# Attention with mxfp4 gate on one core: transposes moved from TensorE to DMA, scores two steps ahead, mask and maximum in one operation

## What is computed

```
xn = layernorm(x)
q, k, v = split(xn @ Wqkv.T + b)            # 16 q heads, 8 k heads, v as 4 x 256, head size 128
p1 = softmax(causal(q[...,0] k[...,0]^T / sqrt(128)));  p2 = the same with the odd heads
p = p1 - lam * p2                            # lam from four vectors and lam0
o = p @ v;  o = o * rsqrt(mean(o*o) + eps) * subln * (1 - lam0)
s = o @ out_w.T + out_b
g = silu(quant(xn) @ quant(ffn_w).T + ffn_b) # quant: mxfp4, blocks of 32
out = x + s * g
```

## Time and profile before

| | us |
|---|---|
| median of 3 runs | 1835.9 (1833.76 to 1836.29) |
| the profiled execution, whole | 1837.28 |
| its span | 1835.5 |
| granted TensorE clock, mean | 0.977 |
| one batch of 32 steps in the middle | 213.50 |
| PE, DVE, ACT, POOL busy | 1678.7, 1269.1, 964.5, 710.0 |

### The profile page before, as it was taken

One profiled execution on the slowest core, in us unless ns is written; L12 is line 12 of the kernel. 1 busy time (PEld: TensorE's weight loads), 2 busy tenths in 40 slices (PEclk: granted clock), 3 DMA queues, 4 the chain that ended last, 5 costly groups with the idle time before them and its releaser, 6 DMA issues.

```text
span 1835.5 us, 29927 instructions
## 1 busy us (share of the span) xinstructions
PE 1678.7 (91%) x10545; PEld 1039.1 (57%) x10577; DVE 1269.1 (69%) x2829; ACT 964.5 (53%) x2642; POOL 710.0 (39%) x1442
## 2 busy tenths in 40 slices
PE   3568999999899999999999999999989999999988
PEld 2345565556655565556655566555655566556654
DVE  4668888548874688648884588646885488845772
ACT  4554566436653566436664366534664366634661
POOL 2214553226422463225532364224632255323243
PEclk7879999999999999999999999999999999999999
DMA  7300000100000000100001000010001000000001
GB/s 258 92 24 1 1 1 1 52 18 1 1 30 30 12 1 1 41 24 7 1 4 49 18 2 1 29 35 7 1 1 41 24 7 1 7 24 24 1 1 40
DMA packets 20680, 42.04 MB, mean 23 GB/s; under 512 B 1682, under 2 KB 2228, under 8 KB 20532
## 3 DMA queue, kind: packets, MB, share of 16 engines
q1 hardware_dynamic: 20532, 40.13, 6.5%
HBM read 31.74 MB, written 8.39 MB: 22 GB/s over the span
## 4 chain that ended last, share of the span: by engine, by line
PE 37%; DVE 28%; ACT 15%; issue 12%; POOL 6%; DMA 0%; SPq 0%; POOLq 0%; DVEq 0%; ACTq 0%
PE ps L418 11%; PE ps L420 10%; PE ps L419 10%; ACT pp L654 9%; DVE negmax L922 6%; DVE pp L937 4%; DVE qkv L879 4%; DVE ps L920 2%; DVE coef L935 2%; DVE ebias L925 1%; ACT qkv L632 1%; PE ps L542 1%; PE ps L474 1%; DVE v L889 1%; PE ps L476 1%
## 5 line engine op out<-in xcount | busy, mean ns | idle before, releaser
L654 ACT ACTIVATE pp<-ps,ebias,ssc 128x384 f32<-128x384 f32 (+3 forms) x512 | 312.1, 614 | 289.2 <-DVE ebias L925 229.7
L418 PE MATMUL ps<-xT,wqkv 128*128 128x512 f16 x768 | 295.2, 384 | 8.5 <-DVE qkv L879 5.3
L419 PE MATMUL ps<-xT,wqkv 128*128 128x512 f16 x768 | 294.4, 383 | 0.0
L420 PE MATMUL ps<-xT,wqkv 128*128 128x512 f16 x768 | 294.3, 383 | 0.0
L700 ACT ACTIVATE junk<-ps 128x256 bf16<-128x256 f32 x256 | 98.0, 383 | 270.4 <-PE ps L420 270.3
L418 PE MATMUL ps<-qkv,pT 128*128 128x256 f16 x640 | 175.2, 274 | 56.8 <-issue 41.0
L922 DVE TENSOR_REDUCE negmax<-ps 128x2 f32<-128x256 f32 (+3 forms) x256 | 211.1, 824 | 8.8
L911 DVE SCALAR_TENSOR_TENSOR res<-ps,small,obias 128x512 f32<-128x512 f32 x32 | 24.0, 751 | 249.0 <-PE ps L420 249.0
L418 PE MATMUL ps<-wout,heads 128*128 128x512 f16 x512 | 194.0, 379 | 0.0
L419 PE MATMUL ps<-wout,heads 128*128 128x512 f16 x512 | 194.0, 379 | 0.0
L420 PE MATMUL ps<-wout,heads 128*128 128x512 f16 x512 | 194.0, 379 | 0.0
(11 more groups left out here) (150 smaller groups left out, 3768.0 us busy)
## 6 DMA issues: line engine op xcount, KB each, us to landing
xin<-in_L_attn_hidden_states SPq DMA_DIRECT2D x8, 1024.0 KB, 5.3
xres<-in_L_attn_hidden_states SPq DMA_DIRECT2D x32, 256.0 KB, 2.8
out_x<-res SPq DMA_DIRECT2D x32, 256.0 KB, 2.0
qkv<-in_L_attn_Wqkv_w SPq DMA_DIRECT2D x8, 512.0 KB, 9.7
heads<-in_L_attn_Wqkv_w SPq DMA_DIRECT2D x8, 512.0 KB, 11.5
qkv<-in_L_attn_out_w SPq DMA_DIRECT2D x4, 512.0 KB, 3.8
heads<-in_L_attn_out_w SPq DMA_DIRECT2D x4, 512.0 KB, 3.6
gate<-in_L_ffn_weight SPq DMA_DIRECT2D x1, 1024.0 KB, 13.2
```

Of the source, the lines that this page charges most:

```text
L418: mm(out, ah, bh, start=start and j == 0, stop=False)
L419: mm(out, ah, bl, start=False, stop=False)
L420: last = mm(out, al, bh, start=False, stop=stop and j == n - 1)
L654: run(pp[:, m, 0:w], sc_ps[:, m, 0:w], ACT.Exp, bias=ebias[:, m:m + 1], scale=ssc[:, c:c + 1], accum_out=psum_l[:, s % 2, m:m + 1]).then_i ...
```

## The change

Six things are done together.

1. TensorE turns neither the map nor the output. The combined map is split in two fp16 parts first (`ph`: high on ACT, low on DVE, from SBUF), and SP issues a transposing DMA of 128 x 2w fp16 elements into `pT`. The output is also split first (`on`: high and low, the low part a new DVE operation each step), and a second transposing DMA of 128 x 512 fp16 elements puts it into `oT`. The copies from PSUM of the turned output (L663, L943) are gone. 512 transposing DMAs of 64 to 256 KB stand in SP's queue, two a step.
2. Scores run two steps ahead instead of one. The two banks that held the turned map and output are a second scores buffer.
3. Mask, scale and maximum are one DVE operation per map (two a step), with a bf16 mask as wide as the map: `tensor_tensor_reduce`, which the build turns into two instructions each, the second a 128x1 write of the result.
4. The second exponential is written back over its scores in PSUM, and `combine` reads it there.
5. Row sums, norms and square sums have two or four buffers; POOL forms its first two norm values two steps ahead.
6. The gate's t1, t2 buffers are replaced by `gate` and `v32`, so the v fill also waits for the gate. Stores and residual loads have fixed places between the transposing DMAs on SP.

```diff
-            def maxima(g, s, step):
-                diag = sc_ps[:, :, w - P:w]
-                tt(diag, diag, mask[:].unsqueeze(1).broadcast_to([P, 2, P]), ALU.add).then_inc(mask_done, 1)
-                nc.vector.tensor_reduce(out=negmax[:], in_=sc_ps[:, :, 0:w], axis=AX.X, op=ALU.max, negate=True)
-                tt(ebias[:], negmax[:], ssc[:, c:c + 2], ALU.mult).then_inc(ebias_done, 1)
+            def maxima(n, m):
+                dve.wait_ge(scores_done, n + 1)
+                sc = sc_ps[u][:, m, 0:w]
+                nc.vector.tensor_tensor_reduce(sc, sc, mask[:, S - w:S], ssc[:, c:c + 1], BIG, ALU.add, ALU.min,
+                                               ebias[:, u, m:m + 1]).then_inc(max_done, 1)
...
+            def transpose_p(n):
+                w = place(n)[3]
+                wait(sp, ph_lo, n + 1)
+                wait(sp, pv_done, n - 1)
+                sp.dma_start_transpose(pT[:, n % 2, 0:2 * w // P, :], ph[:, n % 2, 0:2 * w])\
+                  .then_inc(pT_done[n % 2], 16)
+            def transpose_o(n):
+                wait(sp, on_lo, n + 1)
+                sp.dma_start_transpose(oT[:, c:c + 2, :, i * P:(i + 1) * P].rearrange("p c s t -> p (c s) t"),
+                                       on[:, h].rearrange("p c s t -> p (c s t)")).then_inc(oT_done[h], 16)
...
+            for n in range(NSTEPS):                       # PE
+                if n + 2 < NSTEPS:
+                    scores(n + 2)
+                for f in PLAN[n]:
+                    fill(f)
+                attend(n)
...
+            for n in range(NSTEPS):                       # ACT
+                if n:
+                    square_o(n - 1)
+                if n + 1 < NSTEPS:
+                    p_hi(n + 1)
+                if n:
+                    normalised(n - 1)
+                if n + 2 < NSTEPS:
+                    exps(n + 2)
+                for f in PLAN[n]:
+                    fill(f)
...
+            for n in range(NSTEPS):                       # DVE
+                    combine(n + 1)
+                    maxima(n + 2, 1)
+                    p_lo(n + 1)
+                    maxima(n + 2, 0)
+                prepare_some(b, s, 0)
+                    normalised_lo(n - 1)
+                prepare_some(b, s, 1)
+                for f in PLAN[n]:
+                    fill(f)
+                prepare_some(b, s, 2)
```

More of the change, by code:

```diff
@@ L108, with plan, place, fill_of @@
 PROLOGUE = [("xT", 0, k) for k in range(NT)] + [(kind, 0, j) for kind, j in PROJ]
[L109 to L113, removed]
+Fill = namedtuple("Fill", "kind g j n hi v ffn gate out")
+def plan():
+    n = hi = v = ffn = 0
+    rows = []
+    for b in range(-1, B):
+        steps = schedule(b > 0, b < B - 1) if b >= 0 else [PROLOGUE]
+        for step in steps:
+            row = []
+            for kind, g, j in step:
+                gate = 4 * b + j
+                out = 4 * b + (j if kind == "last" else j - NT)
+                row.append(Fill(kind, g, j, n, hi, v, ffn, gate, out))
+                n += 1
+                hi += kind in ("q", "k", "xT")
+                v += kind == "v"
+                ffn += kind == "ffn"
+            rows.append(row)
+    return rows[0], rows[1:], n
+FIRST, PLAN, FILLS = plan()
+assert len(FIRST) % 2 == 0
+END = [Fill("out", 0, k, FILLS + k - (NT - 2), 0, 0, 0, 0, (B - 1) * NT + k) for k in (NT - 2, NT - 1)]
+NSTEPS = B * NS
+def place(n):
+    return n // NS, n % NS // STEPS, n % STEPS, (n % STEPS // 2 + 1) * P
+def fill_of(kind, b, g, j):
+    rows = [FIRST, *PLAN]
+    lo = max(0, b * NS + 1 - (NS // 4 if g == 0 and kind in ("q", "k", "v", "xT") else 0) - (2 if kind == "xT" else 0))
+    for row in rows[lo:lo + NS + NS // 4]:
+        for f in row:
+            if (f.kind, f.g, f.j) == (kind, g, j):
+                return f.n
+    raise KeyError((kind, b, g, j))
 WB = 2 * NC * G
@@ L130, in setup_order @@
             i += 1
[L131 to L157, removed]
+    return order + [("fill", m) for m in range(i, len(PROLOGUE))] + [("scores", 0)] + [("o", n) for n in range(OB)] \
+        + [("ahead", 0)]
 def build(nc, x_d, wqkv_d, bqkv_d, lq1_d, lk1_d, lq2_d, lk2_d, sub_d, ow_d, ob_d, fw_d, fb_d, out_d):
@@ L407, in _ @@
+            transpose_o(NSTEPS - 1)
+            for k in range(1, NT):
+                if k > 1:
+                    residual(B - 1, k)
+                store(B - 1, k)
             sp.wait_ge(res_free, 16 + 16 * B * NT)
@@ L1032, in _ @@
+            normalised_lo(NSTEPS - 1)
+            for f in END:
+                fill(f)
         @block.gpsimd
@@ L1170 @@
+            norm_of(NSTEPS - 1)
+            for f in [*PLAN[NSTEPS - 1], *END]:
+                if f.kind == "out" or f.kind == "last" and LAST_PIECES[f.j][f.g][1] == OC:
+                    finish(f)
 _INS = ["L0_attn_hidden_states", "L0_attn_Wqkv_w", "L0_attn_Wqkv_b", "L0_attn_lambda_q1", "L0_attn_lambda_k1",
```

574 lines of the change are left out of this document (260 added, 314 removed).

## The result

The changed kernel takes 1777.1 us (median of four runs, 1774.2 to 1780.7), the kernel before 1836.0 in the same comparison: a ratio of 0.968 (95% interval 0.966 to 0.971), 59 us less. The forecast was 1808 us, 28 less. The sign and the range were right, the size was half of what came. The profiled execution of the changed kernel is the slowest of its four, 1780.7 us, so profiles show a gain of 57 us and not of 59.

A forecast was written before the change was run, and what follows sets the result against it. PE's queue was taken to bound 79 us of each batch and a DVE and ACT lap 135 us. From 1837.3, 28 less for transposes and 0 for the rest gave 1809, median 1808 us; range 1770 to 1880.

The forecast's parts named there:

- The transposes: PE's queue in each batch's first stretch (steps 0 to 7): 36 fewer at 0.11 us, 28 us over seven batches.
- The lap: Once-a-step DVE and ACT loop outside the first stretch: 3.77 us plus two maxima at w = 384, +0.21 us a lap.
- the exponential's price: One exponential on the DVE and ACT loop: 0.71 us, half of the earlier 1.42, and 0.09 to reach it.
- the term on contention: POOL holding DVE operations with two SBUF operands, L925 gone but new coefficient added: +0.08 us a lap, +2 us a batch.
- The last batch: Had no term of its own; counted among seven batches gaining 4.0 us each from first-stretch transposes.
- The three other stretches: Rest of each batch after steps 0 to 7: +3.8 laps, -5.8 preparation, +2 contention, sum 0.
- the preparation in shadow: Slot 1 of the quantisation preparation moves off the loop, behind the maxima beside ACT's work: 5.8 us a batch saved.
- the maximum is dear: Rival 1: joined maximum costs 0.81 us instead of 0.59, +42 us, 1850 us; chance 0.14.
- turned maps land late: Rival 2: transposing DMAs land too late in short steps, 1866 us, chance 0.11; queue-bound at 3277 us, chance 0.05.
- the lap opens: Third rival: two steps of lookahead free PE, the three later stretches shrink towards PE's work, 1704 us; chance 0.07.
- What would show it: Signs of being right: first stretch about 75 us, others 47, 44, 44, no PE in their chain, DMAs 2 to 3 us.
- The other signs of being wrong: PE waiting for turned maps over 20 us a batch; DVE over 95% busy in the last three stretches.

The follow-up runs named there:

- Kernel 5: Changed kernel with mask, maximum and scale as three separate operations per map again, exponential's scale read from SBUF: 1929.4 us.
- kernels 8 and 9: Changed kernel, for map n+2 at the end of step n: 8, reciprocal alone behind DVE's fills, 1791.8 us; 9, reciprocal and coefficient ahead of them, 1762.6 us.
- Kernel 3: Changed kernel with the exponentials' scale of -1.0 read from a column of SBUF instead of a constant: 1789.2 us.
- Kernel 4: Changed kernel with the second map's exponential written to a buffer in SBUF and read there by the combination: 1797.4 us.
- kernel 11: Changed kernel with both the exponentials' scale from a column of SBUF and the second map's exponential in SBUF: 1811.0 us.
- kernel 12: Changed kernel with scale from SBUF, second exponential in SBUF, and 144 TensorE transposes of the identity per batch put back: 1841.9 us.
- kernels 1: Changed kernel with 144 unread TensorE transposes of the identity per batch put back, in all stretches: 1804.0 us.
- kernel 7: Changed kernel with each transposing DMA of the probabilities preceded on the same queue by another of the same size into an unread buffer: 1794.1 us.
- kernel 10: Kernel 9 with the combination's result written over the first map's scores in PSUM, high and low parts made from there: 1735.0 us.

## Why the prediction was right or wrong

**The transposes** were right: 28 us forecast, 27 measured, all but 1.4 of it by those of the first stretch, at the 0.11 us of the earlier trace rows.

**The lap** was right as a path and, by a coincidence, to 0.01 us. Kernel 5 shows that both maxima stand on it, kernels 8 and 9 that reciprocal, coefficient and the fill's low part do. Of its links the reciprocal took 0.11 us with its hand-over (forecast 0.19), the coefficient 0.25 (0.29), the combination 0.65 (0.61), the link beside the first maximum 0.65 (0.59, and it is the map's high part that sets it), the low part 0.62 (0.54), the second maximum 0.63 (0.59), and the exponential with its read 0.67 (0.80).

**The step that failed first is the exponential's price.** The prediction took half of the earlier trace rows's 1.42, so the old form. The diff turns its scale from a tile into a constant, and that is 90 ns for each exponential. Kernel 3 puts it at 12 us.

**The second is the term on contention.** The prediction looked for it at L925 and at the new coefficient alone, in the earlier trace rows, and took +2 us a batch, 16 in all. Over the shortest of its shape L925 stood at 39 us and the coefficient stands at 40, so this pair changed nothing in DVE's own time. Two others did change. The combination's operand moved from SBUF to PSUM, and with that 17 us of being held went. The map's low part read PSUM before (L1006, 2 us over its shortest) and now reads two operands in SBUF: 34 us. The prediction priced both near their shortest, 0.61 and 0.54. Kernel 4 puts the combination's place at 20 us, in the new order. The mean of 638 ns of L937 at 384 columns hid it; at 128 columns the mean was 510 for a shortest of 350, and I had not looked at that width.

Kernels 3 and 4 together are 32 us, and kernel 11, with both undone, stands at 1811 where the forecast was 1808. So the 12 us of the scale are shown as what the forecast lacked. For the rest of the gap, 19 us, the close agreement is in part luck: in kernel 11 the combinations are held for 30 us, in the kernel before they were for 17, and the forecast had neither. That the operand's place is worth 20 us in the new order is shown; that it brought as much against the kernel before is not.

**The last batch** was priced like any other, at 4.0 us, and gave 18.6. Of that, 8.1 are the three parts (kernel 12's 192.6 less 184.5): 5 to 7 the transposes, 1 to 3 the two others, by kernels 1 and 11. The remaining 10.5 stay in every version with the new order. They are balanced by what the same order costs in the other batches, and that is luck: it is why the total of kernel 11 fits a forecast that had neither. Whether they come from the second step of lookahead, from the turns by DMA, or from the residuals' loads, which the new code issues earlier, was not taken apart. My first reading, that the last batch gained by the combination no longer being held, fell with kernel 4 (1.5 us).

**The three other stretches** were to balance: +3.8 for the laps, -5.8 for the preparation in shadow, +2 for contention. In kernel 11, whose exponential is as the forecast took it, they take 134.4 us a batch, cut at PE's matmuls and in the mean of six, and 133.5 before: 0.9 more. The first stretch is 76.2 us there and 79.9 before, 3.7 less, where its transposes are 3.9. So the sum of zero held to 1 us a batch; how its three parts came out no run shows. (Cut at ScalarE's squares, as in the table, kernel 11 has 137.4 for 133.6 in them and 73.5 for 79.6 in the first: some nine matmuls of the fills, 2 us, change sides there.)

**The rivals.** That the maximum is dear did not happen: 0.61 us of DVE's time in the lap. That turned maps land late did not either, at 2.7 us; kernel 7 shows that it was nearer than the forecast had it, 17 us for a landing 1.4 us later. What the prediction did not have at all is the 1.2 us for which each transposing DMA keeps SyncE, 2.5 us of every step. The rule of the Trainium skill that speaks against the change (VectorE: DVE Perf Modes, "The three transpose paths") compares single blocks. Here two to eight go in one DMA, the median lands in 2.7 us beside other work, and a plain store of 256 KB in 2.3; TensorE's 0.11 us a block is still the shorter time, as the Trainium skill has it, but the preference for it does not hold here, because TensorE's time is on the path in the first stretch and the DMA's is not. The second place cited in the prediction (the Trainium skill, Advanced Engine Details and Errata, "X-Bar Transpose (TRN2)"), by which turning DMAs are as fast as others, agrees better with the 2.7 against 2.3 us. Its 350 GB/s give an estimate of 1.1 us, not under 1, for the 384 KB of a step with 512 columns. That the lap opens did not happen: DVE, ACT and their waits still set the last two stretches. What no rival had is POOL's queue in the second and third stretch.

**What would show it**: the first stretch near 75 us, no PE in the lap, the pair near 0.6 us and landings of 2 to 3 us were all met. The last two stretches at 44 were not, and this was the sign of terms left out. The last of them, at 41.79, even met the sign of the third rival (under 42), although DVE and ACT still set it. The other signs of being wrong stayed away: PE waited for landings for 6 us a batch and not 20, and DVE was busy for 83 to 87% of these stretches and not 95.

## What to carry to other kernels

When a change rewrites an operation, price each operand anew, by its kind (constant or tile) and its place (SBUF or PSUM), even where the operation does the same; undoing two such details cost 34 us here, more than the 36 transposes on the path. A stretch that is cut at one engine's instruction takes that engine's delays with it: cut it at the engine whose work is being counted. Where a kernel has a lap between two in-order engines, write down its links in queue order first, and move work ahead of the instruction that waits, not behind it. And read the contention from the shortest and the mean of every width, since the mean of one width can hide it.

## What the hardware showed that was not expected

- The combination with one input in PSUM was never held by GpSimd: 256 combinations within 4 ns of the shortest of their width, against single ones of up to 1.8 us with both in SBUF, each of them beside a GpSimd operation of 256 or 512 elements. Keeping the combined map in PSUM, for its high and its low part (kernel 10), brought 27.6 us.
- A transposing DMA keeps SyncE for 1.2 us, a store of 256 KB for 0.34 (kernel before). Two in a row overlap after that: the second is issued 1.25 us behind the first and lands 2.9 us later, where one alone took 2.7.
- An exponential is 27 ns shorter with its result in PSUM and 90 ns shorter with a constant scale (384 columns).
- The joined operation costs as much as a plain one of its width (617 ns at 384, as the combination), and its result needs a second instruction of 141 ns.
